# Piecewise-linear softmax: the score clamp and the scaling by the reciprocal on GpSimd

## What is computed

```python
def pla_softmax(scores):
    m = jnp.max(scores, axis=-1, keepdims=True)
    shifted = to_fixed_point(scores - m, 32, 26)
    xc = jnp.clip(shifted, -10.0, 0.0)
    idx = jnp.clip(jnp.searchsorted(PLA_A, xc, side='right') - 1, 0, PLA_A.shape[0] - 2)
    exps = PLA_M[idx] * xc + PLA_C[idx]
    sm = exps / (jnp.sum(exps, axis=-1, keepdims=True) + 1e-09)
    return quant(to_fixed_point(sm, 16, 15))
```

## Time and profile before

| | us |
|---|---|
| median of 3 runs | 2284.58 (2279.36 to 2289.71) |
| the profiled execution | 2280.63 |
| its span on the core | 2278.9 |
| outside the span | 1.7 |

### The profile page before, as it was taken

The page is one execution under the profiler, slowest core; times in us unless marked ns, Lnnn a source line. Parts: engine busy times, 40 slices in busy tenths (PEclk is TensorE's granted clock), DMA queues, the critical chain, the costliest instruction groups (busy, mean ns, idle before and its releaser), DMA issues. The chain is left out here.

```text
span 2278.9 us, 36311 instructions
## 1 busy us (share of the span) xinstructions
PE 1683.8 (74%) x12222; PEld 1362.8 (60%) x12238; DVE 1253.7 (55%) x2614; ACT 1053.5 (46%) x2190; POOL 416.9 (18%) x551
## 2 busy tenths in 40 slices
PE   3699969958824499876499676664984798489995
PEld 2366658646613255565499444443773697479995
DVE  6488853351167799968423659997217211633223
ACT  4578743323335588864122248873422354422221
POOL 0342100007710000001242100000000332034431
PEclk9799969879965699987799887775996799789998
DMA  4200010216530000003465100000004553357775
GB/s 86 75 20 20 22 27 3 66 37 177 168 114 1 6 6 6 3 2 87 150 226 183 66 4 8 7 3 1 13 8 127 156 185 124 115 176 225 221 214 193
DMA packets 137248, 189.86 MB, mean 83 GB/s; under 512 B 51661, under 2 KB 111213, under 8 KB 137069
## 3 DMA queue, kind: packets, MB, share of 16 engines
q1 hardware_dynamic: 116289, 146.91, 21.1%
q0 software_dynamic: 15360, 36.72, 5.6%
q10 hardware_dynamic: 5420, 3.91, 0.7%
HBM read 150.21 MB, written 33.68 MB: 81 GB/s over the span
## 5 line engine op out<-in xcount | busy, mean ns | idle before, releaser
L1014 DVE TENSOR_TENSOR 36_l3f_mlp_hidden<-36_l3f_mlp_gate,36_l3f_mlp_first 128x512 f32<-128x512 f32 x51 | 35.1, 688 | 172.5 <-ACT 36_l3f_mlp_gate L992 105.2
L907 PE MATMUL 36_l3f_mlp_first<-36_l3f_mlp_xT,36_l3f_mlp_w 128*128 128x128 f32 x816 | 100.6, 277 | 0.0
L907 PEld LDWEIGHTS 36_l3f_mlp_first<-36_l3f_mlp_xT,36_l3f_mlp_w 128*128 128x128 f32 x816 | 96.4, 194 | 0.0
L1309 PE MATMUL 2_performer_p_u<-perf_proj,2_performer_yT 128*87 128x512 f32 (+1 forms) x204 | 84.5, 554 | 7.3 <-DVE 2_performer_arg L1470 6.2
L992 ACT ACTIVATE 36_l3f_mlp_gate<-36_l3f_mlp_first 128x512 f32<-128x512 f32 x51 | 30.5, 597 | 115.2 <-PE 36_l3f_mlp_first L912 115.2
L1030 DVE TENSOR_SCALAR 9_l0f_mlp_y<-9_l0f_mlp_second,l0f_routing_weight 128x192 f32<-128x192 f32 x51 | 21.3, 418 | 112.2 <-DMA l0f_results<-9_l0f_mlp_y,l0f_routing_put 81.2
L1028 DVE TENSOR_TENSOR 32_l3a_mlp_y<-32_l3a_mlp_second,l3a_experts_b_rows 128x192 f32<-128x192 f32 x29 | 10.4, 358 | 130.2 <-issue 95.6
L921 PE MATMUL 36_l3f_mlp_second<-l3f_experts_w,36_l3f_mlp_hidden 128*128 x408 | 79.9, 339 | 0.0
L2671 ACT ACTIVATE l1a_p<-14_pla_f,l1a_recip 128x87 int16<-128x87 f32 x272 | 71.7, 353 | 9.2 <-DVE l1a_recip L2746 9.2
L988 ACT ACTIVATE 32_l3a_mlp_hidden<-32_l3a_mlp_first,l3a_experts_b_cols 128x128 f32<-128x128 f32 x174 | 48.1, 375 | 60.1 <-PE 32_l3a_mlp_first L912 59.9
L1014 DVE TENSOR_TENSOR 22_l1f_mlp_hidden<-22_l1f_mlp_gate,22_l1f_mlp_first 128x512 f32<-128x512 f32 x29 | 20.0, 688 | 99.7 <-ACT 22_l1f_mlp_gate L992 99.7
(11 more groups left out here) (933 smaller groups left out, 4948.4 us busy)
## 6 DMA issues: line engine op xcount, KB each, us to landing
36_l3f_mlp_w<-in_L_ffn_w_dram SPq DMA_DIRECT2D x51, 768.0 KB
22_l1f_mlp_w<-in_L_ffn_w_dram SPq DMA_DIRECT2D x29, 768.0 KB, 5.0
32_l3a_mlp_w<-in_L_attn_W_dram SPq DMA_DIRECT2D x29, 576.0 KB, 3.9
9_l0f_mlp_w<-in_L_ffn_down_w_dram SPq DMA_DIRECT2D x51, 192.0 KB
l3a_experts_w<-in_L_attn_W_dram SPq DMA_DIRECT2D x8, 576.0 KB, 8.3
l1a_blocks<-l1a_qkb SPq DMA_DIRECT2D x192, 5.4 KB, 1.8
l1f_experts_w<-in_L_ffn_w_dram SPq DMA_DIRECT2D x8, 384.0 KB, 6.2
l2a_blocks<-l2a_qkb SPq DMA_DIRECT2D x192, 5.4 KB, 1.8
```

Of the source, the lines that this page charges most:

```text
L907: nc.tensor.matmul(to(t + a * PAIRS), of[:, t + a * PAIRS, :], at[:, 0, :], start=(t == 0), stop=True, skip_group_check=True)
L1014: v.tensor_tensor(hidden[j % 2][:], gate[j % 2][:], first[j % 2][1][:, 0, 0:HT, :], ALU.mult).then_inc(hidden_done, 1)
L1309: ins = t.matmul(p_u[:, k, 0:(EIGHT - h) * M], yT[b % 2][:, k, :], proj[:, h:EIGHT, :].rearrange("p h m -> p (h m)"), start=True, stop=True)
```

## The change

The clamp of every unit moves from VectorE to GpSimd, and so does the share-out, from ScalarE. The arithmetic is the same. The two functions stand now in GpSimd's list, which in turn j does the clamp of unit j + 2 and then the share-out of unit j. ScalarE's list loses the share-out and its last two turns; VectorE's list loses the clamp.

```diff
         @block.gpsimd
         def _(pool):
...
+            g = nc.gpsimd
+
+            def clamp(j):
+                pool.wait_ge(raw_ready, j + 1)
+                g.tensor_scalar(less, raw[:], HOME, LEAST_V, ALU.add, ALU.max).then_inc(less_ready, 1)
+
+            def share_out(j):
+                pool.wait_ge(recip_ready, j + 1)
+                for n in range(CHUNKS):
+                    ins = g.tensor_scalar(P[:, j, n, :], f[j % 2][:, n * NT:(n + 1) * NT], recip[:, j, n:n + 1], None, ALU.mult)
+                ins.then_inc(stored, 1)
+
+            for j in range(-2, U):
+                if has(j + 2):
+                    clamp(j + 2)
+                if has(j):
+                    share_out(j)
+            pool.wait_ge(stored, U)
...
-            def share_out(j):
-                act.wait_ge(recip_ready, j + 1)
-                for n in range(CHUNKS):
-                    ins = a(P[:, j, n, :], f[j % 2][:, n * NT:(n + 1) * NT], ACT.Copy, scale=recip[:, j, n:n + 1])
-                ins.then_inc(stored, 1)
...
-            for j in range(-2, U + 1):
+            for j in range(-2, U - 1):
                 if has(j + 1):
                     count_steps(j + 1)
-                if has(j - 1):
-                    share_out(j - 1)
-                if has(j + 1):
                     move_high(j + 1)
                 if has(j + 2):
                     take(j + 2)
-            act.wait_ge(stored, U)
...
-            def clamp(j):
-                dve.wait_ge(raw_ready, j + 1)
-                v.tensor_scalar(less, raw[:], HOME, LEAST_V, ALU.add, ALU.max).then_inc(less_ready, 1)
...
             for j in range(-2, U):
-                if has(j + 1):
-                    clamp(j + 1)
                 if has(j):
                     cut(j)
```

## The result

The changed kernel takes 2380.2 us, median of six runs (2375.1 to 2400.9), beside 2286.4 for the kernel before, median of six (2279.4 to 2294.3): ratio 1.0428, 95% interval 1.0400 to 1.0457. Forecast were 2302 us, range 2284 to 2332: the sign was right, the size (+18) five times too small.

The account below looks back on a forecast made before the run. VectorE and TensorE were taken to bound the softmax stage together, 12.05 us a turn. Turns +12.4, end load +4.8 and last share-out +0.6 gave +17.8 us: 2302 us against the median 2284.58, range 2284 to 2332.

Parts of the forecast that it names:

- The prices on GpSimd: GpSimd in the softmax stage: clamp 1.7 us (1.41 to 3.29), one share-out 0.3 us (0.25 to 0.37), 5.1 per unit.
- And no bound by itself: Clamp and 17 share-outs put 6.8 us a turn on GpSimd, so GpSimd alone would not bound the stage.
- The rival in which GpSimd becomes the bound: Clamp, share-outs and waits fill GpSimd's turn: 11.9 us, with upper prices 14.7, 2326 us; chance 0.14 with the dear clamp.
- the dear clamp: Clamp on GpSimd at its upper price, 3.29 us: turn 14.6 us, +33; chance 0.14 together with GpSimd as bound.
- signs of being wrong: Cut at 1.69 without wait, clamp far from 1.7, share-outs over 0.4 us each, or the load at the end hidden.
- Who meets whom: GpSimd's clamp and VectorE's cut come at the same moment; the cut waits for all of it: turn 13.0 us, +12.4.
- TensorE's clock falls: Rival: TensorE pauses 1.98 us a turn, its clock drops, up to 1.77 us per fall; 2314 or 2325 us; chance 0.12.
- The clamp leaves VectorE: VectorE loses 0.84 us between reciprocal and cut, all on the path: turn 11.21 us, -10.9 over 13 turns.
- The share-out leaves ScalarE: ScalarE loses 4.48 us lying beside VectorE's cut, search and shift; costed at nothing inside a turn.
- The load at the start: Load at the softmax stage's start, finished before the first clamp: costs nothing, up to 7.6 us if uncovered.
- The load at the end: Load ahead of the maximum, behind the barrier, with every engine waiting: +4.8 us, bounds 4.8 to 6.6.
- The last share-outs: The last unit's share-out, exposed at the stage's end, takes 5.1 instead of 4.48 us: +0.6, between -0.2 and +1.8.

Follow-up runs that it names:

- the probe: Kernel before plus a stage behind the softmax that only measures GpSimd operations; with VectorE idle the clamp's form takes 5.21 us, a share-out 0.515.
- clamp ahead: Kernel before with only the clamp on GpSimd, two raw-score buffers, and scores, maxima and take one unit further ahead; 2352.6 us, ratio 1.0306.
- the added reduction: Changed kernel plus one one-input VectorE reduction a turn, 128 x 1479, on tiles of its own; 2376.7 us, ratio 1.0395 to the kernel before.
- one product alone: Kernel before with only the share-out on GpSimd, as one two-tensor product, and a ScalarE copy to 16-bit integers; 2382.2 us, ratio 1.0396.
- half the clamp: Changed kernel with GpSimd clamping 740 of 1479 columns and VectorE the other 739; 2365.4 us, ratio 1.0328 to the kernel before.

## Why the prediction was wrong

- **The prices on GpSimd: this step failed.** "I take 1.7 us, near the copy, and 0.3 us for one share-out": measured 5.22 and 0.515, both above the upper bounds of 3.29 and 0.37 too. The bounds came from a copy and an addition of two tensors, on the idea that an operation with one input lies between them; the probe puts one and two operations per column above both. The estimate of 1.3 to 2.2 us worked out from the Trainium skill ("GPSIMD Engine Reference", section 3.1) failed alike; its upper end takes for an ordinary loop what that page calls a best case. That page's two-input figure, some 2.6 cycles per element, gives an estimate of 3.2 us for 1479 columns, and the probe's product of two tensors takes 3.30.
- **"And no bound by itself": wrong through the prices.** The rival in which GpSimd becomes the bound had the right terms. With 5.22 for 1.7, 8.35 for the share-outs' 5.1 and 4.1 for up to 5.1 of waits, its 11.9 becomes 17.7; 17.83 was measured. It was given 0.14 together with the dear clamp, and its 2326 rested on prices still too low. Of the signs of being wrong that the prediction named, three came: the cut at 1.64 with no wait ahead of it, the clamp far from 1.7, and share-outs over 0.4.
- **Who meets whom: right as a mechanism, absent where it was forecast.** With GpSimd as the bound the clamp comes behind the cut and seldom meets it; only once in 16 turns did the second half wait (5.51). Where GpSimd is not full, the mechanism acts as described: 4.15 for the cut beside the product, 5.29 beside the clamp ahead, with the pause of TensorE and the fall of its clock, a rival here, on top. That a one-input GpSimd operation blocks at all, left open by the rows, is so: 5.50 for 1.69 in the probe. The Trainium skill, "SBUF — State Buffer", section "Who interferes with whom", says that a VectorE instruction with two SBUF inputs contends with a GpSimd instruction that reads SBUF, and that `tensor_reduce` does not; the traces agree on both, the added reduction having cost nothing.
- **TensorE's clock falls, a rival:** it fell (4.97 us of pause, then 4.12 for six products), but GpSimd set the turn. The prediction took from the earlier trace rows that a pause of 1.95 us is enough. Its length alone does not decide: after 1.95 us six products took 4.12 there and 2.44 with one product alone (at 1038.06), and after 2.66 us they took 4.11 and 2.46 with the clamp ahead (at 815.71 and 892.80).
- **The clamp leaves VectorE, -0.84 a turn:** the time came free but nothing used it; VectorE waits 6.99 instead.
- **The share-out leaves ScalarE, at nothing:** right for the order of before. With the share-outs alone on GpSimd, the first five turns, in which VectorE does not yet wait for GpSimd, take 12.05 to 12.14. With the clamp alone on GpSimd, though, its 4.48 lie in the loop that sets the turn.
- **The load at the start,** nothing: right (loaded at 769.9, first clamp at 782.4). **The load at the end,** +4.8: 5.1. **The last share-outs,** +0.6: 4.7, by the same price.

## What to carry to other kernels

Price an operation on another engine by a row of the same operation there; where there is none, "one input" or "looks like a copy" is no bound, and an engine whose price is unknown by a factor of three must be counted as a possible bound with its waits. Before moving work to GpSimd, ask three things apart: does its load fit in the turn, does its duration stand on the path, and which VectorE operation begins just behind it, those with two inputs above all; the last was cured here by short pieces, not by less work. Sometimes the same step a few instructions later on the old engine is the better move.

## What the runs showed of the hardware

- GpSimd's tensor_scalar: 2.53 ns a column for one operation, 5.23 us for two over 1479 columns, beside 1.42 for a copy and 2.66 for a product with a repeated column.
- Waiting is not always for the whole instruction. Behind the product the cut still needed 1.55 us (907.21 to 908.76), nearly all of its own 1.64; behind the clamp ahead it ended after 0.36 (905.02 to 905.38), so by these rows some 1.3 us of it ran while the clamp did.
- The stage behind the softmax can keep the lower clock to its end. Busy time by stretch, the first 15 us of that stage in the changed kernel and, with the clamp alone, in the other case:

```profile
1082.40:1087.40 5.00, 1.54 (x15) 1.54 (x16) 2.91 (x8) 0.00 (x0) 0.38 (x1) 0.50 0.00 0
1087.40:1092.40 5.00, 4.63 (x70) 4.41 (x68) 2.19 (x4) 4.14 (x7) 0.00 (x0) 0.71 0.02 3
1092.40:1097.40 5.00, 4.78 (x101) 4.63 (x100) 4.32 (x10) 4.74 (x7) 0.00 (x0) 1.00 0.00 0
```

```profile
1052.55:1057.55 5.00, 1.55 (x15) 1.56 (x16) 2.91 (x8) 0.00 (x0) 0.38 (x1) 0.50 0.00 0
1057.55:1062.55 5.00, 4.63 (x51) 4.41 (x50) 1.49 (x3) 4.09 (x6) 0.00 (x0) 0.50 0.01 3
1062.55:1067.55 5.00, 5.00 (x58) 5.00 (x56) 2.98 (x7) 2.10 (x3) 0.00 (x0) 0.50 0.00 0
```

  The first 5 us are alike; then the clock goes from 0.50 to 1.00 within some 10 us, or stays at 0.50 though TensorE is busy for 4.63 and 5.00 of 5 us, and the stage takes 64.9 us instead of 44.6. What decides between the two stays open: TensorE's pause ahead of the stage was 20.1 us here and 24.7 in the changed kernel, but also 20.3 in a run in which the clock rose (clamp ahead) and 25.8 in one in which it did not (half the clamp).
